# GpSimd's products of an attention step gated on the scaled probabilities, with four smaller moves, in a two-layer attention and feed-forward kernel

## The reference, cut to what matters

```python
# block 1, attention of 32 heads of 128; keys and values come from ctx
x   = rmsnorm(layernorm(x)) ;  q, k, v = x @ w_q.T, ctx @ w_k.T, ctx @ w_v.T
s   = softmax(where(mask, q @ k.T + position_bias, -inf))
x1  = x + hidden + (s @ v) @ w_out.T
# block 2, a feed-forward of 1376 with 8-bit fake quantisation of rows and tokens
x2  = x1 + qlinear(silu(qlinear(y, w_gate)) * qlinear(y, w_up), w_down)   # y = layernorm(x1)
# block 3: the 76 largest of 128 context values per position (top) split layernorm(x2) in two
# branches, whose maxima and means over the tokens feed a 7-tap convolution and a sigmoid
# block 4: a router over 8 low-rank experts, the two best per token
```

## Time and profile before

| | us |
|---|---|
| median of 3 runs (lowest, highest) | 1130.93 (1130.86, 1132.14) |
| the profiled execution's own time | 1132.07 |
| its span in the trace | 1130.3 |
| TensorE busy | 1008.1 (89%) |
| VectorE, ScalarE, GpSimd busy | 779.4, 516.1, 485.4 |
| TensorE's mean granted clock | 0.958 of full |
| DMA, mean over the span | 77 GB/s |

### The profile page before, as it was taken

The page is one execution under the profiler, slowest core; times in us unless marked ns, Lnnn a source line. Parts: engine busy times, 40 slices in busy tenths (PEclk is TensorE's granted clock), DMA queues, the critical chain, the costliest instruction groups (busy, mean ns, idle before and its releaser), DMA issues. The chain is left out here.

```text
span 1130.3 us, 18395 instructions
## 1 busy us (share of the span) xinstructions
PE 1008.1 (89%) x5994; PEld 846.7 (75%) x6010; DVE 779.4 (69%) x1850; ACT 516.1 (46%) x1330; POOL 485.4 (43%) x364
## 2 busy tenths in 40 slices
PE   3799999999999999998999999989999999465465
PEld 2688788888888888887888888878888877333353
DVE  6686777777777777786765676685585675588384
ACT  2354444444444444445543553544544354167251
POOL 4545544444444444444444443454363452334200
PEclk8899999999999999999999999999999999798577
DMA  6133333333333333313322222222222210000002
GB/s 211 57 91 93 93 92 91 91 91 117 99 94 100 97 99 106 94 46 120 105 85 75 79 81 79 80 80 63 66 80 79 81 61 22 19 1 1 0 1 75
DMA packets 50354, 87.58 MB, mean 77 GB/s; under 512 B 6320, under 2 KB 15152, under 8 KB 50288
## 3 DMA queue, kind: packets, MB, share of 16 engines
q1 hardware_dynamic: 50288, 86.76, 24.7%
HBM read 84.64 MB, written 2.10 MB: 77 GB/s over the span
## 5 line engine op out<-in xcount | busy, mean ns | idle before, releaser
L540 POOL TENSOR_TENSOR b_mask<-b_raw,mask_add 128x512 f32<-128x512 f32 x64 | 82.2, 1284 | 178.6 <-DMA b_raw<-in_bias 130.5
L1448 PE MATMUL pX<-wv_lo,cT_hi 128*128 128x256 f32 x512 | 149.1, 291 | 0.7 <-ACT v_sb L659 0.7
L1450 PE MATMUL pX<-wv_hi,cT_hi 128*128 128x256 f32 x512 | 143.8, 281 | 0.0
L1449 PE MATMUL pX<-wv_hi,cT_lo 128*128 128x256 f32 x512 | 143.6, 280 | 0.0
L1156 DVE TENSOR_TENSOR score<-pS,b_mask 128x512 f32<-128x512 f32 x64 | 44.2, 691 | 143.5 <-PE pS L1624 143.5
L792 ACT ACTIVATE prob<-score,neg_max 128x128 f32<-128x128 f32 x256 | 99.7, 391 | 78.2 <-DVE neg_max L1159 78.0
L532 POOL TENSOR_TENSOR wv_lo<-raw_v,wv_hi 128x1024 fp32r<-128x1024 f32 x32 | 77.6, 2424 | 131.2 <-ACT wv_hi L659 131.2
L532 POOL TENSOR_TENSOR wk_lo<-raw_k,wk_hi 128x512 fp32r<-128x512 f32 x64 | 83.2, 1301 | 85.9 <-ACT wk_hi L659 85.9
L659 ACT ACTIVATE v_sb<-pX 128x512 f32<-128x512 f32 x64 | 38.2, 597 | 176.4 <-PE pX L1450 176.4
L1448 PE MATMUL pX<-xT_lo,wq_hi 128*128 128x512 f32 x256 | 107.0, 418 | 4.3 <-DVE xT_lo L984 4.3
L532 POOL TENSOR_TENSOR wo_lo<-raw_o,wo_hi 128x512 fp32r<-128x512 f32 x64 | 85.0, 1328 | 59.5 <-ACT wo_hi L659 59.3
(11 more groups left out here) (273 smaller groups left out, 2443.2 us busy)
## 6 DMA issues: line engine op xcount, KB each, us to landing
raw_q<-in_wq SPq DMA_DIRECT2D x64, 256.0 KB, 5.9
raw_k<-in_wk SPq DMA_DIRECT2D x64, 256.0 KB, 5.6
raw_v<-in_wv SPq DMA_DIRECT2D x32, 512.0 KB, 7.3
raw_o<-in_wo SPq DMA_DIRECT2D x64, 256.0 KB, 2.7
b_raw<-in_bias SPq DMA_DIRECT2D x64, 64.0 KB, 5.8
g_raw<-in_w_gate SPq DMA_DIRECT2D x16, 172.0 KB
f_raw<-in_w_down SPq DMA_DIRECT2D x4, 688.0 KB, 4.1
g_raw<-in_w_up SPq DMA_DIRECT2D x16, 172.0 KB
```

The lines of the kernel that those rows point to most:

```text
L540: g.tensor_tensor(b_mask[:], b_raw[:].to_broadcast([P, HB, S]), mask_add[:, half * HB:(half + 1) * HB, :], ALU.add).then_inc(s_b_mask, 1)
L1448: mm(dst, lh, rl, start=start, stop=False, skip_group_check=lint)
L1449: mm(dst, ll, rh, start=False, stop=False, skip_group_check=lint)
L1450: return mm(dst, lh, rh, start=False, stop=stop, skip_group_check=lint)
```

## The change

GpSimd's step now begins with `early_rsqrt`, then waits for `s_norm_done` of the same step, and then makes wq_lo, b_mask, wo_lo and wk_lo in this order. ScalarE's integers of the hidden layer move from the end of step r = 4 to step r = 5, behind the exponentials. VectorE's maxima of the branches move from `early_bubble` of step r = 11 to `early_end` of the same step. `residual(0)` moves from the end of step 32 to right behind the scaling of step 32.

```diff
@@ GpSimd
             def step(n, m, odd, half):
+                early_rsqrt(n)
+                pool.wait_ge(s_norm_done, n + 1)
+                if unless_last(n + 2):
+                    lo("q", n + 2)
                 if unless_last(n + 1):
                     bias_mask(n + 1, (n + 1) // H if isinstance(n, int) else half)
-                if unless_last(n + 2):
-                    lo("q", n + 2)
                 lo("o", n)
                 if unless_last(n + 2):
                     lo("k", n + 2)
-                early_rsqrt(n)
                 if odd and unless_last(n + 3):
                     lo("v", m + 2)
                 early_split(n)
@@ ScalarE
+            def early_hidden(n):
+                t = turn(n, 5)
+                if t is not None:
+                    act.wait_ge(s_e_h_mag, t + 1)
+                    a.activation(e_hq[:], e_gate[:], ACT.Copy, bias=-MAGIC).then_inc(s_e_h_q, 1)
...
-                t = turn(n, 4)
-                if t is not None:
-                    act.wait_ge(s_e_h_mag, t + 1)
-                    a.activation(e_hq[:], e_gate[:], ACT.Copy, bias=-MAGIC).then_inc(s_e_h_q, 1)
...
                 e.then_inc(s_exp_done, 1)
+                early_hidden(n)
                 if unless_last(n + 1):
                     query_out(n + 1)
@@ VectorE: out of early_bubble, into early_end behind e_gate
                 t = turn(n, 11)
                 if t is not None and t < EARLY_Z:
                     dve.wait_ge(s_e_split, t + 1)
                     for br in range(2):
                         last = v.tensor_reduce(stat[0][:, :, br, t:t + 1], e_split[:, br], AX.X, ALU.max)
                     last.then_inc(s_e_maxed, 1)
@@ VectorE: step
                                 ALU.mult).then_inc(s_norm_done, 1)
                 early_first_bank(n)
+                if isinstance(n, int) and n == H:
+                    residual(0)
                 if j == 0:
...
                     add_norm(n // (H - 1))
-                if isinstance(n, int) and n == H:
-                    residual(0)
```

More of the change, by code:

```diff
@@ L1075, in early_bubble @@
                                     ALU.subtract, ALU.mult).then_inc(s_e_z_t, 1)
[L1076 to L1081, removed]
             def early_first_bank(n):
@@ L1108, in early_end @@
                     v.tensor_scalar(e_gate[:], e_up[:], e_hs[:, 2:3], MAGIC, ALU.mult, ALU.add).then_inc(s_e_h_mag, 1)
+                t = turn(n, 11)
+                if t is not None and t < EARLY_Z:
+                    dve.wait_ge(s_e_split, t + 1)
+                    for br in range(2):
+                        last = v.tensor_reduce(stat[0][:, :, br, t:t + 1], e_split[:, br], AX.X, ALU.max)
+                    last.then_inc(s_e_maxed, 1)
                 t = turn(n, -2)
```

## The result

The changed kernel takes 1142.63 us (median of 4 runs, 1140.67 to 1145.68) against 1130.89 for the kernel before in the same sitting: a ratio of 1.0096, 95% interval 1.0075 to 1.0117. It is 11.7 us slower. Measured once more among the experiments (e12) it stands at 1.0104, interval 1.0084 to 1.0124. The profiled execution took 1142.36 us with a span of 1140.6; before it was 1132.07 and 1130.3.

What follows compares the result with a forecast made beforehand. TensorE bounds the kernel; with the gate a ring through g_raw's load would bind in steps 6 to 31. Sum: -3.0 + 8.5 - 2.9 + 2.1 + 1.5 = +6.2 us on 1130.93, so 1137.1 us, range 1125 to 1147.

Steps and rivals of the forecast that it cites:

- The ring: Steps 6 to 31: scaling, q, mask, o products, g_raw's issue, landing, rows of g, scaling; 14.06 us a step, +8.5 us.
- the landing: Link from g_raw's issue to VectorE having it, steps 6 to 31: 6.25 us into even steps, 6.9 into odd.
- The even steps: Even steps of 6 to 31 lose 0.16 us each to contention now; without a binding g_raw loop, 26 x (13.745 - 13.64).
- rival 1: Steps 6 to 31: g_raw's loop does not bind, landing 5.7 us on average; -5.0 us, 1125.9 us; chance 0.20.
- Steps 0 to 5: Start of the kernel: scaling freed from GpSimd's products brings step 5's transposes from 130.7 to 127.6, -3.0 us.
- Steps 32 and 33: Residual moved behind the scaling of step 32 no longer holds back step 33's score and TensorE: -2.9 us.
- 0.8 for a later product with v: Steps 32 and 33: the moved residual pushes back pick and the copies, so TensorE's product with v comes 0.8 us later.
- 19.48 - 15.8: Step 33: 19.48 us long before, 15.8 with the residual moved; less 0.8 it gives the -2.9 us.
- The power's wait: Steps 36, 42, 48, 54: early_rsqrt, ahead of all products, waits for e_ve; 1.0, 3.05, about 3.5 each: +11.0 us.
- What stands against it: Steps 42, 48, 54, 60: 1.1 us each; maxima in 49, 55: 1.45 each; late low part and p copies: together -8.9.
- Clock: New TensorE waits of 2.5 to 3 us may lower its clock, 1.5 us each; one fall taken, +1.5; three +4.5.
- Rival 2: More hangs on g_raw's loop: wq_hi, pick meeting GpSimd, late p's copy; 0.3 us more a step, 1145 us; chance 0.15.

Runs made afterwards that it cites:

- e12: The changed kernel measured once more, unedited, as a control: 1143.25 us, 1.0104 of the kernel before.
- e1: The changed kernel with Sync issuing g_raw of the next step ahead of raw_o instead of behind it: 1128.62 us, 0.9965 of before.
- e6: The changed kernel with g_raw's 86 rows loaded by two transfers, of 80 and 6 rows, queue order as changed: 1128.52 us, 0.9972 of before.
- e9: The kernel before with g_raw issued ahead of raw_o and GpSimd's wait for s_norm_done as the only part of the change: 1118.33 us, 0.9895.
- e2: The kernel before, without the change, with g_raw issued ahead of raw_o: 1127.73 us, 0.9965 of before.
- e3: The changed kernel without GpSimd's wait for the scaling; order of products and the other moves stay: 1134.00 us, 1.0021 of before.
- e7: e5 with the first residual back at the end of step 32, its place before the change: 1120.65 us, 0.9899 of before.
- e4: The changed kernel with early_rsqrt (the power) back behind the product of k: 1133.50 us, 1.0015 of before.
- e8: e5 with the branch maxima and the hidden layer's integers back in their places before the change: 1120.12 us, 0.9900 of before.
- e5: The changed kernel with g_raw issued ahead of raw_o and early_rsqrt back behind the product of k: 1121.50 us, 0.9902 of before.

## Why the prediction was right, and where it was not

It said 1137.1 us, within 1125 to 1147, slower; 1142.63 came. Its points in its own order:

- **The ring** holds, link by link, and the two ways of opening it (e1, e6) each take the loss away. The predicted steps of 14.0 to 14.1 us are 14.22. The term that was mis-sized is the landing: 6.25 into even steps and 6.9 into odd ones were two single rows, and the 26 steps show 6.53 and 6.96, from 6.13 to 7.46. That is 0.17 us on average, 26 x 0.17 = 4.4, against 4.1 missing in the window (365.6 predicted, 369.7 measured). The rest of the ring was right: 14.22 - 6.75 = 7.47 a step measured, 14.06 - 6.58 = 7.48 predicted.
- **The even steps** were to gain 0.16 each if the ring were open (rival 1, with 13.64 for TensorE alone). TensorE alone takes 13.73: e9 against e2 shows 0.55 us in 26 steps, not 2.7.
- **Steps 0 to 5**: -3.0 predicted, -2.0 measured. With the ring open it is -3.6 (e1), of which the issue order alone gives 2.0 (e2). The ring had taken back more than the worked chain allowed.
- **Steps 32 and 33**: -2.9 predicted, -0.6 measured (32.16 against 32.78): step 33 is 1.3 us shorter, step 32 is 0.7 longer, and that 0.7 goes with the ring: in e1, e3 and e6 step 32 lasts 13.3 us as before, so the 0.8 for a later product with v is not there either. The failed step is "19.48 - 15.8". Moved away, the residual uncovers f_raw's integers, which still hold the score back, so that the move is worth 1.0 us (e7); and TensorE's remaining wait was again followed by the lower clock, another 1.5, which 15.8 takes as gone. The outputs of step 33 now start at 523.70 behind a wait of 2.17 us, where it was 3.75:

```profile
520.68 0.94 DVE L1133 TENSOR_SCALAR f_raw<-f_raw,f_s 128x1376 f32<-128x1376 f32 x1
521.53 0.69 DVE L1161 TENSOR_TENSOR score<-pS,b_mask 128x512 f32<-128x512 f32 x1
...
522.92 0.68 DVE L1156 TENSOR_TENSOR aT_lo<-pT,aT_hi 128x512 fp32r<-128x512 f32 x1
...
523.70 0.47 PE L1453 MATMUL oacc<-wo_lo,aT_hi 128*128 128x512 f32 x1 [2.17 <-issue]
```

- **The power's wait**: predicted 11.0 us, 6.0 by e4, which is the term's real size. Step 36 is as said (1.0 predicted; step 37 is 1.04 shorter in e4). 42 gave 2.1 instead of 3.05, 48 and 54 gave 1.0 and 2.1 instead of 3.5. TensorE waits as predicted (8.5 us in steps 37, 43, 49 and 55), but without the power ahead it waits in or next to the last three of these too, 0.6 to 1.0 us for aT_lo and in step 48 1.5 for p's copy (e4). That the gate's products are late by themselves is shown by e9, which has these waits as well (0.57 to 1.03, and 1.53 in step 48).
- **What stands against it**: predicted -8.9. e4 against before in steps 34 to 62 shows -3.8. Steps 42, 54 and 60 are 1.0 shorter each, close to the 1.1 predicted, but 43 is 0.9 longer, where TensorE now waits for aT_lo, and 61 is 0.6 longer; 48 and 49 together save 1.4 and 55 saves 0.4, against the 1.45 each for the maxima and what was added for 48; and the maxima's move is worth nothing with the gate in place (e8). Both terms were about twice too large, and that their difference came out (+2.1 predicted, +2.25 measured over steps 34 to 62) is luck.
- **Clock**: one more fall was allowed for, +1.5. There was none in the profiled execution of the changed kernel, nor in those of e12 and e1, which have the same waits. The term's size was right all the same: e3's execution has all three falls, in steps 43, 49 and 55, and pays 4.7 us for them, where "three would be +4.5". That none came in this execution is as much chance as forecast. The only attention step below full is 33, which before had a fall as well (0.58 from 513 to 517):

```profile
523.00:527.00 4.00, 3.30 (x10) 2.60 (x11) 2.57 (x11) 2.13 (x10) 0.00 (x0) 0.70 0.73 254
```

- **Rival 2** named the mechanism of the k copy and priced it beside the ring, at 1145. It is there, 8.6 us in eight places, but inside the ring: e1 and e6 end both with one edit, save 2 us in steps 0 and 4. That the time came near its 1145 is owed to the landing and not to this.
- **Rival 1** fell with the landing: it needed 5.7 us on average.

Up to step 63 the sum is -2.0 + 12.35 - 0.6 + 2.25 = +12.0, and 0.7 for a later start. Against the prediction's +6.2 that is 6.5 more: 3.85 in the ring (12.35 against 8.5), 2.3 in steps 32 and 33, 1.0 in steps 0 to 5, 0.15 in the second half and the 0.7, less the 1.5 for the clock.

## What to carry to other kernels

A wait put in front of one engine's work to spare another must be followed through every queue it feeds: here the bill came from a DMA that the change does not name, because it stands in an in-order queue behind one that waits for the gated product. Open that ring first (issue ahead of the waiting load, or give the transfer a number of rows that many engines can share), and the same gate turns from a cost into a gain: taking it out of the changed kernel gained 0.75% (1.0096 to 1.0021, e3), putting it in behind the exchanged issues gained 0.7% (0.9965 to 0.9895, e9).

When TensorE pays a long ring, look at the step that pays, not at the link that is slow: the waits pointed at k's copy, and they went with an edit of Sync's order that touches neither the copy nor pick (e1). An edit of pick or of the copy was not run; by the ring's 14.22 us, in which neither stands, it would not have been the cure. And a duration that enters a sum 26 times should be averaged over as many rows as the trace has, not read from two. When two traces are compared by steps, the granted clock of each step is compared first: a step of 19.92 us and one of 17.50 differed here by the clock and not by the edit.

## What was not expected of the hardware

- Two transfers of 43 rows land in 9.88 us on average where one of 86 takes 6.75; 80 and 6 let the transfers behind them land 2 us sooner (5.9 to 3.9).
- The same wait of TensorE in step 33 (2.04 us in e8, 2.05 in e5) is followed by a granted clock below full in one execution and not in another. The stretches of e8 and e5 from the start of step 33:

```profile
501.30:520.00 18.70, 16.66 (x100) 14.15 (x100) 11.61 (x31) 8.40 (x20) 4.91 (x4) 0.91 0.32 113
```

```profile
502.30:520.00 17.70, 15.65 (x102) 13.45 (x102) 12.16 (x31) 8.83 (x20) 4.87 (x4) 1.00 0.31 107
```

Step 33 lasts 17.97 and 16.43 us. 1.5 us of any difference there is this and not the edit. The length of the wait does not decide it: e9 waited 3.03 us in step 33 and stayed at the full clock, and e3 and the changed kernel differ in the same way in steps 43, 49 and 55. What decides it stays open.
- A VectorE instruction with a single input in SBUF was held up by a GpSimd product: f_raw's integers, 3.10 us instead of 0.94. The prediction had only the two-input case. The Trainium skill (SBUF — State Buffer, "Who interferes with whom") allows it: `tensor_scalar` can enter a mode that takes the shared pair of ports, and then blocks against GpSimd.

Open is why g_raw landed 0.11 us sooner on average in e4.
